# One queue's work dealt to another: SP issues three loads and all stores, ACT issues the later loads between its copies

## The reference

```
x:        128 x 128 x 1024, float32       (samples b, channels c, time t)
subjects: 128 integers from 0 to 7
weights:  8 x 128 x 128, float32
w   = weights[subjects]
out = x + einsum('bct,bcd->bdt', x, w)
```

## Time and profile before

| what | value |
|---|---|
| time, median of 3 runs | 323.60 us (323.48 to 323.99) |
| the profiled execution, its own time | 323.66 us |
| its span, first to last instruction | 321.7 us |
| mean granted TensorE clock | 0.892 |
| busy: PE / DVE / ACT | 249.0 / 196.3 / 132.3 us |
| moved by DMA | 134.82 MB, mean 419 GB/s over the span |

### The profile page before, as it was taken

The page is one execution under the profiler, slowest core; times in us unless marked ns, Lnnn a source line. Parts: engine busy times, 40 slices in busy tenths (PEclk is TensorE's granted clock), DMA queues, the critical chain, the costliest instruction groups (busy, mean ns, idle before and its releaser), DMA issues.

```text
span 321.7 us, 2829 instructions
## 1 busy us (share of the span) xinstructions
PE 249.0 (77%) x1024; PEld 114.8 (36%) x1024; DVE 196.3 (61%) x261; ACT 132.3 (41%) x131; POOL 0.8 (0%) x7
## 2 busy tenths in 40 slices
PE   0698929888975969969597796978949599599920
PEld 0343504344432424434242342434414244244410
DVE  3386843868781682838648186483836828368740
ACT  4064622636460552526336063362524525255630
POOL 1000000000000000000000000000000000000000
PEclk9999978999996996979989597797989979699975
DMA  7999999999999999999999999999999999999996
GB/s 287 420 403 430 421 428 428 430 423 427 432 428 425 429 430 426 427 429 429 426 430 429 427 427 428 430 427 428 429 429 426 428 430 427 427 428 429 428 426 259
DMA packets 17590, 134.82 MB, mean 419 GB/s; under 512 B 672, under 2 KB 1200, under 8 KB 1200
## 3 DMA queue, kind: packets, MB, share of 16 engines
q1 hardware_dynamic: 9008, 67.63, 50.1%
q10 hardware_dynamic: 8576, 67.12, 49.3%
HBM read 67.64 MB, written 67.11 MB: 419 GB/s over the span
## 4 chain that ended last, share of the span: by engine, by line
DMA 68%; PE 25%; DVE 2%; issue 1%; DVEq 0%; SPq 0%; ACTq 0%
DMA x_ring<-x 42%; DMA out<-x_ring 26%; PE product L233 25%; DVE x_ring L154 1%; DVE x_ring L153 0%; DVEq L54 0%; SPq L94 0%; DVEq L141 0%; ACTq L202 0%
## 5 line engine op out<-in xcount | busy, mean ns | idle before, releaser
L233 PE MATMUL product<-x_ring,weight_ring 64*128 64x512 f32 x1024 | 249.0, 646 | 59.0 <-DMA x_ring<-x 45.9
L233 PEld LDWEIGHTS product<-x_ring,weight_ring 64*128 64x128 f32 x1024 | 114.8, 206 | 192.3 <-issue 154.9
L153 DVE TENSOR_TENSOR x_ring<-product,x_ring 64x1024 f32<-64x1024 f32 x64 | 77.9, 1217 | 104.6 <-PE product L233 104.6
L196 ACT COPY x_ring<-product 64x1024 f32<-64x1024 f32 x64 | 64.5, 1008 | 173.5 <-PE product L233 173.5
L154 DVE TENSOR_TENSOR x_ring<-product,x_ring 64x1024 f32<-64x1024 f32 x64 | 78.6, 1228 | 0.8
L197 ACT COPY x_ring<-product 64x1024 f32<-64x1024 f32 x64 | 64.2, 1003 | 0.8
L141 DVE COPY weight_ring<-weight_bank 64x256 f32 x128 | 36.9, 288 | 3.9 <-issue 1.0
L188 ACT COPY weight_bank<-weight_halves 64x1024 f32<-64x1024 f32 x2 | 2.2, 1112 | 2.2 <-DMA weight_halves<-weights 2.2
L158 DVE TENSOR_SCALAR subject_row<-subject_row 1x128 int32<-1x128 int32 x1 | 0.2, 215 | 3.7 <-DMA subject_row<-subjects 3.7
L122 DVE COPY weight_bank<-weight_halves 64x1024 f32<-64x1024 f32 x2 | 1.4, 688 | 0.9 <-DMA weight_halves<-weights 0.9
L188 ACT ACT_TABLE_LOAD x1 | 1.3, 1283 | 1.3 <-PEq L249 1.3
## 6 DMA issues: line engine op xcount, KB each, us to landing
x_ring<-x SPq DMA_DIRECT2D x14, 4096.0 KB, 29.8
out<-x_ring ACTq DMA_DIRECT2D x13, 4096.0 KB, 29.5
x_ring<-x SPq DMA_DIRECT2D x4, 2048.0 KB, 16.6
out<-x_ring ACTq DMA_DIRECT2D x6, 1024.0 KB, 11.2
out<-x_ring ACTq DMA_DIRECT2D x3, 2048.0 KB, 16.9
weight_halves<-weights SPq DMA_DIRECT2D x1, 512.0 KB, 4.0
subject_row<-subjects ACTq DMA_DIRECT2D x1, 8.0 KB, 2.9
```

The costliest lines, as they stand in the source:

```text
L153: dve.tensor_tensor(x_ring[LOW, slot, 0, :], low[LOW, :], x_ring[LOW, slot, 0, :], add)
L196: act.copy(x_ring[LOW, slot, 1, :], low[HIGH, :])
L233: last = pe.matmul(product[slot % PRODUCTS][a][:, cols], weight_ring[half, slot, r, :], x_ring[half, slot, r, cols], start=r == 0, stop=r ...
```

## The change

The list of loads is cut in two. SP issues the weights, x0, x2 and x4 (now two tiles), and then all 22 stores, each behind the same waits for `copied` and `summed` as before. ACT issues the rest: x6 (two tiles, with a new semaphore `x_fourth`), x8 and x12 behind tile 0's copies, and from tile 16 on one place ahead: ahead of the copies of tile 12 it waits for `x_out` of place 0 and issues x16, ahead of tile 16's x20, and so on to x60 and x62 ahead of tile 56's. Ahead of tile 4's copies ACT waits for x6, since PE's tile 6 reads it. Numbers of transfers and of bytes: one load more (x4 is split), the same bytes. The arithmetic on all engines is the same.

```diff
--- before.py
+++ after.py
@@ -7,7 +7,6 @@
 DMA_INC = 16
 SLOTS = 16
 PLACE = 4
-LOADS_AHEAD = 3
 PICK_AHEAD = 4
 PRODUCTS = 2
 
@@ -32,7 +31,8 @@
     assert TILES % SLOTS == 0 and SLOTS % PLACE == 0 and SLOTS % PRODUCTS == 0 and PICK_AHEAD > PRODUCTS
     PLACES = SLOTS // PLACE
 
-    LOADS = ((0, 2), (2, 2), *((tile, PLACE) for tile in range(PLACE, TILES - PLACE, PLACE)), (TILES - 4, 2), (TILES - 2, 2))
+    SP_LOADS = ((0, 2), (2, 2), (4, 2))
+    ACT_LOADS = ((6, 2), *((tile, PLACE) for tile in range(2 * PLACE, TILES - PLACE, PLACE)), (TILES - 4, 2), (TILES - 2, 2))
     STORES = ((0, 1), (1, 1), (2, 2), (4, 2), (6, 2), *((tile, PLACE) for tile in range(2 * PLACE, TILES - PLACE, PLACE)),
               *((tile, 1) for tile in range(TILES - PLACE, TILES)))
     BANKS = T // PSUM_BANK_COLS
@@ -78,6 +78,7 @@
         x_out = [ctx.enter_context(nc.semaphore(f"x_out{s}")) for s in range(PLACES)]
 
         x_second = ctx.enter_context(nc.semaphore("x_second"))
+        x_fourth = ctx.enter_context(nc.semaphore("x_fourth"))
         x_last = ctx.enter_context(nc.semaphore("x_last"))
 
         picked = ctx.enter_context(nc.semaphore("picked"))
@@ -88,23 +89,29 @@
 
         copied = ctx.enter_context(nc.semaphore("copied"))
         block = ctx.enter_context(nc.Block())
+
+        def load(engine, tile, count):
+            slot = tile % SLOTS
+            landed = {2: x_second, 6: x_fourth, TILES - 2: x_last}.get(tile, x_in[slot // PLACE])
+            engine.dma_start(x_ring[:, slot:slot + count, :, :].rearrange("p s r t -> p s (r t)"),
+                             x_of_tile[:, tile:tile + count, :]).then_inc(landed, DMA_INC)
 
         @block.sync
         def _(sp):
             sp.dma_start(weight_halves[:, :, :, :],
                          weights.rearrange("(i a) (h r) d -> (a h) i (r d)", a=2, r=R)).then_inc(weights_in, DMA_INC)
-            for i, (tile, count) in enumerate(LOADS):
-                slot = tile % SLOTS
-                place = slot // PLACE
-                if tile >= SLOTS:
-                    sp.wait_ge(x_out[place], stores_before(tile - tile % PLACE, place) * DMA_INC)
-                elif i == LOADS_AHEAD:
-                    sp.wait_ge(x_in[0], DMA_INC)
-                elif i > LOADS_AHEAD:
-                    sp.wait_ge(x_second, DMA_INC)
-                landed = x_second if tile == 2 else x_last if tile == TILES - 2 else x_in[place]
-                sp.dma_start(x_ring[:, slot:slot + count, :, :].rearrange("p s r t -> p s (r t)"),
-                             x_of_tile[:, tile:tile + count, :]).then_inc(landed, DMA_INC)
+            for tile, count in SP_LOADS:
+                load(sp, tile, count)
+            for first, count in STORES:
+
+                sp.wait_ge(copied, first + count + PRODUCTS)
+                sp.wait_ge(summed, first + count + PRODUCTS)
+                slot = first % SLOTS
+                sp.dma_start(out_of_tile[:, first:first + count, :],
+                             x_ring[:, slot:slot + count, :, :].rearrange("p s r t -> p s (r t)")).then_inc(
+                    x_out[slot // PLACE], DMA_INC)
+            for place in range(PLACES):
+                sp.wait_ge(x_out[place], DMA_INC * stores_before(TILES, place))
 
         @block.gpsimd
         def _(pool):
@@ -193,13 +200,10 @@
 
                 low, high = product[slot % PRODUCTS]
                 act.wait_ge(multiplied, tile + 1)
+                if tile + PRODUCTS == 6:
+                    act.wait_ge(x_fourth, DMA_INC)
                 act.copy(x_ring[LOW, slot, 1, :], low[HIGH, :])
                 act.copy(x_ring[HIGH, slot, 0, :], high[LOW, :]).then_inc(copied, 1)
-
-            def whole(tile):
-
-                act.wait_ge(copied, tile + (PRODUCTS + 1))
-                act.wait_ge(summed, tile + (PRODUCTS + 1))
 
             act.dma_start(subject_row[:, :], subjects.rearrange("(one b) -> one b", one=1).broadcast_to(
                 (SUBJECT_ROWS, B))).then_inc(subjects_in, DMA_INC)
@@ -207,16 +211,20 @@
             act.wait_ge(weights_in, DMA_INC)
             bank(HIGH, LOW, EVENS)
             bank(HIGH, HIGH, ODDS).then_inc(bank_high, 1)
-            for first, count in STORES:
-                for tile in range(first, first + count):
-                    cross(tile, tile % SLOTS)
-                whole(first + count - 1)
-                slot = first % SLOTS
-                act.dma_start(out_of_tile[:, first:first + count, :],
-                              x_ring[:, slot:slot + count, :, :].rearrange("p s r t -> p s (r t)")).then_inc(
-                    x_out[slot // PLACE], DMA_INC)
-            for place in range(PLACES):
-                act.wait_ge(x_out[place], DMA_INC * stores_before(TILES, place))
+            for tile in range(TILES):
+                if tile == 1:
+
+                    act.wait_ge(x_second, DMA_INC)
+                    for first, count in ACT_LOADS[:3]:
+                        load(act, first, count)
+                elif tile % PLACE == 0 and tile >= SLOTS - PLACE:
+
+                    place = (tile // PLACE + 1) % PLACES
+                    for first, count in ACT_LOADS[3:]:
+                        if first // PLACE == tile // PLACE + 1:
+                            act.wait_ge(x_out[place], stores_before(tile + PLACE, place) * DMA_INC)
+                            load(act, first, count)
+                cross(tile, tile % SLOTS)
 
         @block.tensor
         def _(pe):
```

## The result

| | before | after |
|---|---|---|
| median of 6 runs | 323.43 us | 326.26 us |
| the profiled execution's span | 321.7 us | 324.5 us |
| ratio, 95% interval | | 1.0086 (1.0067 to 1.0104) |

What follows compares the result with a forecast made beforehand. The prediction took the 16 DMA engines, full at 428 GB/s, as the bound. Holes of 4.0 at tile 12, 1.5 after it and 0.6 at the end, 6.1 us, added to 323.66 gave 329.8 us, range 325.8 to 335.

Steps and rivals of the forecast that it cites:

- the first hole: At tile 12, DMA engines idle from 65.3 us until x16 flows at 69.3: 4.0 us, bounds 1.4 to 5.3.
- ACT is free at 49.5 + 18.4 = 67.9, and x16 flows at 69.3: At tile 12: x8 lands at 49.5, its group with copies takes 18.4 us, then x16 needs 1.4 us to flow.
- the row that I had read as costing nothing: First store before, issued 18.18, only 3 packets by 22 us: about 3.8 us, read as other packets going first, price 0.
- the start of 1.4 us: Time from a load's issue until its packets flow, taken as 1.4 us from the weights' 1.3 to 1.5 us.
- A dip well before 65 us: Sign of being wrong: a dip in DMA share beginning well before 65 us, instead of between 65 and 69 us.
- after the hole: Batches behind tile 12: two take at least 39.5 us against 39.4; five holes of 0.3, 1.5 us (0 to 4.5).
- the end: At o56: 20.3 us from x56's landing against 19.7 for the batch before, so 0.6 us (0 to 1.4).
- the rival that ended faster: Lagging DMA engines catch up in a pause and the 20 to 22 us slow spot goes: 322.2 us, chance 0.03.
- Only the first hole: Rival: PE's runs at the short end and batches overlap, leaving 1.4 to 3 us: 325.1 to 326.7 us, chance 0.12.
- Every start costs 3.8 us: Rival: first hole 6.4 us, two batches 41.9, 12.5 for ten batches, end 3: 346 us, chance 0.08.
- No change: Rival: the cushion of loads covers the later issue, needing x8 to land at 45.5: 323.7 us, chance 0.04.
- groups over 20.5 us apart: Sign of being wrong, behind the first hole: groups this far apart would mean the 3.8 us start; 19.7 to 20.1 expected.

## Why the prediction was right or wrong

**Right: what bounds, where, and which way.** The DMA engines were full before; the change takes away the cushion of loads; the first hole comes at tile 12, at 63.5 to 65.5 us. x16 went out at 63.45 us instead of 44.24. The issue instructions and ACT's waits cost nothing, and so did the exchange of queues.

**Wrong: "ACT is free at 49.5 + 18.4 = 67.9, and x16 flows at 69.3".** It was issued at 63.45, 4.4 us sooner. That is the step that failed, in three parts:
- the issue doesn't wait for ACT's copies: 2.0 us (the experiment with that wait put in costs 11 us more than the changed kernel);
- x8 landed at 47.5 and not at 49.5 us: 2.0 us, shown below;
- PE's run at tile 8 was 15.73 us and not 16.2: 0.5 us.

I had let o0 flow at 19.5 us, for it stands behind x4 on its own queue. The DMA queues of the changed kernel from 20 to 22 us (packets, MB, share; q10 is ACT's, which now carries the loads):

```profile
q10 hardware_dynamic: 97, 0.79, 104.6%
```

It fills the engines alone. o0 was issued at 18.50, and SP's queue took part only after 22 us, with the same delay of near 4 us as the first store before. That delay is the row that I had read as costing nothing and then left out for o0. So loads shared their rate no sooner than before, and x8 came on time.

**Wrong size: the hole.** By my own formula an x16 issued at 63.45, flowing at 64.85 with the start of 1.4 us that I took, would leave no hole, for I let the DMA engines run out at 65.3 us. That is when the last laggard is through. Most are done by 63.5: the share there is 0.25. (A dip well before 65 us was one of the signs of being wrong that I had set.) The stretch lost 2.5 us in place of the 4.0 forecast, and the slow spot, of which the sum had no term, is some 0.8 of them.

**Wrong size: after the hole.** 1.5 us forecast, 1.1 us lost (160 to 280 us). The number looks right, but that is luck: two errors nearly cancel. The issue came 16.4 us after the landing two batches earlier (mean of the loads from x24 on), not 18.4, since it doesn't wait for the copies. But from issue to landing a load took some 23.4 us and not 1.4 + 19.7 = 21.1. The pages' rows for the thirteen loads of four tiles have medians (the last figure, us) of 23.8 in the changed kernel and 24.1 with the copies waited for:

```profile
x_ring<-x ACTq DMA_DIRECT2D x13, 4096.0 KB, 23.8
```

```profile
x_ring<-x ACTq DMA_DIRECT2D x13, 4096.0 KB, 24.1
```

So two batches took 39.8 us in the changed kernel, near the 39.5 of the working, and 41.6 with the copies waited for, which is what the working described. That kernel lost 9.1 us from 73 to 280 us where the sum had 1.5. The term that was mis-sized is the time from a load's issue to its landing, by some 2 us. A start beside a busy queue is the likely part of it that I left out (x24: issued at 100.12, its packets from 103.6 us), but no run takes it apart from the slow spots.

**Wrong: the end.** 0.6 us forecast, nothing lost from 280 to 320 us, and 0.7 us gained as the laggards caught up. That was the grain of truth in the rival that ended faster. But its pause is not what does it: with x16 alone held there is the same hole, and the end loses 3.2 us as before. With the later loads as late as in the changed kernel it loses 2.1 to 2.4 us in four runs; why, is open.

**The rivals.** *Only the first hole* (325.1 to 326.7) came nearest: 326.26. PE's run at tile 8 was at its short end, as it says, but that is 0.5 of the 4.4 us by which x16 was sooner. *Every start costs 3.8 us* was half right: not on idle engines (x16 is issued at 63.45, and the share is back at 1.00 from 64.5 us), but starts beside a busy queue took it again. Its two batches of 41.9 us are close to the 41.6 measured where the copies were waited for, and groups over 20.5 us apart, the sign that I had set for it, came there (20.8); in the changed kernel they are 19.9 us apart, for the copies' 2.0 us are missing. *No change* would have needed x8 at 45.5 us; as it turned out, an issue of x16 at 60.4 us is enough.

## What to carry to other kernels

In a kernel that is bound by its transfers, ask of each load not who issues it but when it is handed over, and compare that with when its queue runs dry: until then lateness is free (16 us of it here), and past it 2.5 us of lateness cost some 2. A place in an engine's list is a time only up to that engine's last semaphore wait; to know when a transfer goes out, look for the wait ahead of it, not for the work ahead of it. And read the bytes moved beside the DMA share: a share of 1.0 hid 0.8 us from 67.5 to 70.5 us.

## What the runs showed of the hardware

- ACT's queue issued x16 at 63.45 us, 0.01 us into the first of the two copies that stand ahead of it. With a wait for the copies' semaphore it was issued 0.08 us after the second copy's end (64.17 + 1.00, 65.25). In these runs only a semaphore held a transfer behind work on its own engine.
- From issue to a queue's first packets: some 1.0 us on idle DMA engines (x16, issued at 63.45; share 0.25 up to 64.5 us and 1.00 from there), near 4 us beside a queue that keeps them busy, whether the new one is ACT's (18.18 to 22 us, before) or SP's (18.50 to 22 us, after).
- DMA engines with a share of 1.0 moved 306 to 324 GB/s for some 3 us ahead of a store's first packets, with the load beside it issued to an empty queue; the spot moved with the store's issue. One of 344 GB/s came beside a queue that had not been empty (20 to 22 us, before), and with x16 issued at 60.4 us there was none, so its condition is open.
